# A two-step tanh in the additive attention of a four-layer tower: one ScalarE instruction for 4096 columns, four wide buffers, and one TensorE wait for two steps

## What is computed

```python
k = x @ Wx                                   # (8, 512, 64)
q = x @ Wt
h = jnp.tanh(q[:, :, None, :] + k[:, None, :, :] + bt)   # (8, 512, 512, 64)
e = jnp.exp(jnp.einsum('bijq,qo->bij', h, Wa) + ba[0])
a = e / (jnp.sum(e, axis=-1, keepdims=True) + EPS)
v = jnp.einsum('bij,bjd->bid', a, x)
...
g = jnp.einsum('sd,edh->esh', flat, w_gate)  # the mixture that follows
u = jnp.einsum('sd,edh->esh', flat, w_up)
y = jnp.einsum('esh,ehd->esd', jax.nn.silu(g) * u, w_down)
```

## Time and profile before

| what | value |
|---|---|
| median of 3 runs | 2263.53 us (2260.45 to 2264.91) |
| profiled execution, its own time | 2263.48 us |
| its span, first to last instruction | 2261.7 us |
| busy PE, DVE, ACT, share of the span | 82%, 77%, 58% |
| tanh of 2048 columns (L1944) | 432 instructions |
| the stage's first and last L1944 | start at 700.9 and 1801.8 us |

### The profile page before, as it was taken

The page is one execution under the profiler, slowest core; times in us unless marked ns, Lnnn a source line. Parts: engine busy times, 40 slices in busy tenths (PEclk is TensorE's granted clock), DMA queues, the critical chain, the costliest instruction groups (busy, mean ns, idle before and its releaser), DMA issues. The chain is left out here.

```text
span 2261.7 us, 31852 instructions
## 1 busy us (share of the span) xinstructions
PE 1845.4 (82%) x11804; PEld 950.2 (42%) x11804; DVE 1746.0 (77%) x4911; ACT 1316.9 (58%) x1459; POOL 328.4 (15%) x392
## 2 busy tenths in 40 slices
PE   6999998988766678999899998889999889755930
PEld 3566655766421123344333443333443364333520
DVE  3676557667777789999999999999999889785532
ACT  1222222231226999999999999999999822110410
POOL 6000111010343000000000000000000000057256
PEclk9898998787778899999999999999999999877965
DMA  5501000000001100000000000000000000031732
GB/s 167 182 1 38 18 1 14 1 1 1 1 0 36 66 1 1 1 1 1 1 1 1 1 1 1 1 1 1 1 1 1 1 1 1 0 140 52 229 106 75
DMA packets 39658, 64.98 MB, mean 29 GB/s; under 512 B 7744, under 2 KB 27728, under 8 KB 38736
## 3 DMA queue, kind: packets, MB, share of 16 engines
q1 hardware_dynamic: 30768, 39.86, 5.3%
q0 software_dynamic: 8736, 23.10, 3.3%
HBM read 37.77 MB, written 23.07 MB: 27 GB/s over the span
## 5 line engine op out<-in xcount | busy, mean ns | idle before, releaser
L1944 ACT ACTIVATE KM<-KM 128x2048 f32<-128x2048 f32 x290 | 539.0, 1909 | 8.0 <-DVE KM L1767 8.0
L1767 DVE TENSOR_SCALAR KM<-big 128x512 f32<-128x512 f32 x1160 | 479.5, 479 | 39.3 <-PE bank L2082 33.6
L2082 PE MATMUL bank<-KM,w_a_wa 128*32 128x512 f32 x2736 | 379.1, 628 | 92.4 <-ACT KM L1944 71.0
L191 POOL TENSOR_TENSOR nrstd<-nrstd,minus_half 128x4 f32<-128x4 f32 (+1 forms) x80 | 82.3, 1049 | 1735.7 <-DVE nrstd L168 1735.5
L1944 ACT ACTIVATE aa_args<-aa_args 128x2048 f32<-128x2048 f32 x142 | 266.1, 1910 | 1.5 <-DVE aa_args L1767 1.5
L1767 DVE TENSOR_SCALAR aa_args<-big 128x512 f32<-128x512 f32 x568 | 235.5, 479 | 13.5 <-PE bank L2082 12.9
L2082 PE MATMUL bank<-aa_args,w_a_wa 128*32 128x512 f32 x1360 | 188.8, 629 | 40.7 <-ACT aa_args L1944 26.8
L2082 PEld LDWEIGHTS bank<-KM,w_a_wa 128*32 128x32 f32 x2736 | 54.7, 109 | 243.0 <-ACT KM L1944 140.7
L1941 ACT ACTIVATE KM<-big 128x512 f32<-128x512 f32 x208 | 132.9, 718 | 0.0
L2048 PE MATMUL bank_pair<-XT,rf_wgu 128*128 128x256 f32 x320 | 88.3, 398 | 0.8 <-DVE ST L1839 0.8
L2054 PE MATMUL bank_pair<-XT,rf_wgu 128*128 128x256 f32 x320 | 88.2, 398 | 0.0
(11 more groups left out here) (451 smaller groups left out, 3300.6 us busy)
## 6 DMA issues: line engine op xcount, KB each, us to landing
queues<-zeros SPq DMA_DIRECT2D x1, 8192.0 KB, 24.0
KM<-queues SPq DMA_DIRECT2D x32, 256.0 KB, 3.7
results<-KM POOLq DMA_DIRECT2D x32, 256.0 KB, 3.1
w<-in_w SPq DMA_DIRECT2D x1, 4096.0 KB, 13.1
mf_tv<-in_task_W SPq DMA_DIRECT2D x1, 2048.0 KB, 9.3
la_v<-in_task_W SPq DMA_DIRECT2D x1, 2048.0 KB, 8.0
big<-XN SPq DMA_DIRECT2D x8, 256.0 KB, 2.7
rf_wgu<-in_wgu SPq DMA_DIRECT2D x1, 2048.0 KB, 8.2
```

The costliest lines, as they stand in the source:

```text
L191: self.nc.gpsimd.tensor_tensor(self.m.nrstd[s][:, 0:self.tiles], self.m.nrstd[s][:, 0:self.tiles], self.m.minus_half[:, 0:self.tiles], ALU ...
L1767: last = nc.vector.tensor_scalar(ARG(n, step)[:, cc, :], KU[:, i * T:(i + 1) * T], q, None, ALU.add)
L1944: last = nc.scalar.activation(ARG(n, step), ARG(n, step), ACT.Tanh)
L2082: last = nc.tensor.matmul(m.bank[g][32 * cc:32 * cc + 32, :], w["a_wa"][:, 30 - 2 * k:62 - 2 * k], ARG(n, step)[:, cc, :], start=k == 0, s ...
```

## The change

One ACT instruction now takes the tanh of two steps, an even one and the odd one after it, over 4096 columns. The six buffers of 2048 columns become four of 4096 (`NBUF` = 8 steps). The fourth is where keys and queries used to lie, so keys and queries go to slices of other tiles, the last queries into a tile of zeros that a transfer reads early in the program. ACT raises `th` once for two steps, after both; PE waits for it in even steps only. In the pairs (8, 9), (12, 13) and (16, 17) ACT makes the biased step, then a tanh of 2048 columns for the odd step, then raises `th`; in (22, 23) both are biased. `used` is still raised for each step.

```diff
-    NBUF = 6
+    NBUF = 8
...
-    ARGS = [t[:, 4 * half:4 * half + 4, :] for t in (m.KM[0], m.KM[1], more) for half in range(2)]
-    ARG = lambda n, step: ARGS[(n * CS + step) % NBUF]
+    BOTH = [t[:, :, :] for t in (m.KM[0], m.KM[1], more)] + [m.big[:, o:o + 8 * T].rearrange("p (a t) -> p a t", t=T)]
+    ARG2 = lambda n, step: BOTH[(n * CS + step) // 2 % (NBUF // 2)]
+    ARG = lambda n, step: ARG2(n, step)[:, step % 2 * CG:(step % 2 + 1) * CG, :]
...
-    arg, th, used = sig("arg", CS - len(BIASED)), sig("th", CS), sig("used", CS)
+    arg, th, used = sig("arg", CS - len(BIASED)), sig("th", CS // 2), sig("used", CS)
...
             def tanh(n, i, step):
-                if step in BIASED:
-                    if n * CS + step >= NBUF:
-                        act.wait_ge(used.sem, used.at(n, step - NBUF + 1))
-                    for cc in range(CG):
-                        last = nc.scalar.activation(ARG(n, step)[:, cc, :], KU[:, i * T:(i + 1) * T], ACT.Tanh, bias=query(n, step, cc))
-                else:
-                    act.wait_ge(arg.sem, arg.at(n, args_before(step) + 1))
-                    last = nc.scalar.activation(ARG(n, step), ARG(n, step), ACT.Tanh)
+                if step % 2:
+                    return
+                for k in (step, step + 1):
+                    if k in BIASED:
+                        if n * CS + k >= NBUF:
+                            act.wait_ge(used.sem, used.at(n, k - NBUF + 1))
+                        for cc in range(CG):
+                            last = nc.scalar.activation(ARG(n, k)[:, cc, :], KU[i], ACT.Tanh, bias=query(n, k, cc))
+                plain = [k for k in (step, step + 1) if k not in BIASED]
+                if plain:
+                    act.wait_ge(arg.sem, arg.at(n, args_before(plain[-1]) + 1))
+                    tile = ARG2(n, step) if len(plain) == 2 else ARG(n, plain[0])
+                    last = nc.scalar.activation(tile, tile, ACT.Tanh)
                 last.then_inc(th.sem, 1)
...
+                    if i == PAIRS - 1:
+                        act.wait_ge(m.queues_zero, 16)
...
                     if attention:
-                        pe.wait_ge(th.sem, th.at(n, step + 1))
+                        if step % 2 == 0:
+                            pe.wait_ge(th.sem, th.at(n, step // 2 + 1))
...
+    m.KU = [m.t512c[1][:, 0, :], m.t512c[1][:, 1, :], m.ST[0][:, 2, :], m.ST[1][:, 2, :]]
+    o = NT * (D + 1) + 8 * T
+    m.QU = [m.big[:, o + i * T:o + (i + 1) * T] for i in range(PAIRS - 1)] + [m.zeros[:, :]]
```

More of the change, by code:

```diff
@@ L1014, in retention_and_balanced_experts @@
     AB = m.bank[2:4]
-    o = NT * (D + 1)
-    KU0, QU0 = m.big[:, o:o + T], m.big[:, o + PAIRS * T:o + PAIRS * T + T]
+    KU0, QU0 = m.KU[0], m.QU[0]
     weight = lambda n, e: WT[n // TILES][:, n % NC_ * HE + n // NC_ % HB * E + e:n % NC_ * HE + n // NC_ % HB * E + e + 1]
@@ L1654, in attention_and_experts @@
     o = NT * (D + 1)
-    KU = m.big[:, o:o + PAIRS * T]
-    QU = m.big[:, o + PAIRS * T:o + 2 * PAIRS * T]
+    KU, QU = m.KU, m.QU
     more = ctx.sb("aa_args", [P, 8, T])
-    ARGS = [t[:, 4 * half:4 * half + 4, :] for t in (m.KM[0], m.KM[1], more) for half in range(2)]
-    ARG = lambda n, step: ARGS[(n * CS + step) % NBUF]
+    BOTH = [t[:, :, :] for t in (m.KM[0], m.KM[1], more)] + [m.big[:, o:o + 8 * T].rearrange("p (a t) -> p a t", t=T)]
+    ARG2 = lambda n, step: BOTH[(n * CS + step) // 2 % (NBUF // 2)]
+    ARG = lambda n, step: ARG2(n, step)[:, step % 2 * CG:(step % 2 + 1) * CG, :]
     PROJ = (2, 12, 22)
@@ L1731, in query @@
     def query(n, step, cc):
-        return QU[:, bass.ds(n * P + (step // KS) * GQ + cc * KS + step % KS, 1)]
+        return QU[n // NC_][:, bass.ds(n % NC_ * P + (step // KS) * GQ + cc * KS + step % KS, 1)]
     with nc.Block() as block:
@@ L1766, in arguments @@
                     q = query(n, step, cc)
-                    last = nc.vector.tensor_scalar(ARG(n, step)[:, cc, :], KU[:, i * T:(i + 1) * T], q, None, ALU.add)
+                    last = nc.vector.tensor_scalar(ARG(n, step)[:, cc, :], KU[i], q, None, ALU.add)
                 last.then_inc(arg.sem, 1)
@@ L1955, in project @@
                     act.wait_ge(kq_ps.sem, kq_ps.at(i - 1, 1))
-                    nc.scalar.copy(KU[:, i * T:(i + 1) * T], m.bank[5][:, :]).then_inc(kq_sb.sem, 1)
+                    nc.scalar.copy(KU[i], m.bank[5][:, :]).then_inc(kq_sb.sem, 1)
                     act.wait_ge(kq_ps.sem, kq_ps.at(i - 1, 2))
-                    nc.scalar.activation(QU[:, i * T:(i + 1) * T], m.bank[6][:, :], ACT.Identity, bias=w["a_bt"][:, 0:1]).then_inc(kq_sb.sem, 1)
+                    if i == PAIRS - 1:
+                        act.wait_ge(m.queues_zero, 16)
+                    nc.scalar.activation(QU[i], m.bank[6][:, :], ACT.Identity, bias=w["a_bt"][:, 0:1]).then_inc(kq_sb.sem, 1)
             def iteration(n, i, c, attention=True):
@@ L2782, in build @@
         m = Memory(whole, nc, dram)
+        m.zeros = m.sb("zeros", [P, T])
         workspace(m)
@@ L2786, in build @@
         m.results = nc.dram_tensor("results", (CE * CAP, D), F32).ap()
-        m.zeros = m.sb("zeros", [P, T])
         m.queues_zero = whole.semaphore("queues_zero")
```

## The result

The changed kernel takes 2302.55 us (median of 4, 2301.09 to 2304.16) against 2263.57 before: ratio 1.0167, interval 1.0146 to 1.0188, so 39 us slower. The prediction was 2294, range 2268 to 2318.

What follows compares the result with a forecast made beforehand. A loop of ACT's half and PE's half was taken to bound the stage. 14 periods at +2.15 us (30.1), -0.6 at the start and +1.2 at the end gave +30.7: 2294 us, range 2268 to 2318.

Steps and rivals of the forecast that it cites:

- What bounds the stage: ACT's half, copy to step 24: 23.58 us; PE's half, to step 9's gate: 39.54; then 5.54 to the copy.
- What is saved: On ACT, each merge of two plain tanhs saves 0.09 us; 192 merges are worth 17 us.
- (1): Hand-over at step 24: PE's half begins at 24.76 us after the copy instead of 23.58, +1.18 a period.
- (2): Step 0: the pair (0, 1) is signalled at 16.66 us, PE comes at 16.54; +0.12 a period.
- (3): Steps 12 and 13: PE waits for both before turning the rows; gate to copy 6.39 us against 5.54, +0.85.
- DVE covered: DVE is not on the loop; its closest place, step 27, is covered by 1 us.
- PE's missing waits: Odd steps of PE's half, now without a wait: counted as nothing, up to 0.8 us a period not excluded.
- The rest: Outside the loop: iteration 0 and first half of 1 sum to -0.6 us, end of last iteration +1.2.
- The loop closes 14 times: Each of 14 periods grows by 2.15 us, 68.66 to 70.8, together 30.1 us.
- my case: The main mechanism, the loop lengthened by late signals: 2276 to 2300 us, chance 0.66.
- The clock as a rival: PE's half clock at step 20 falls on steps 22 to 24, 0.7 to 1.6 us each: 2304 to 2316, chance 0.10.
- Every merge counts: Rival: the loop is looser and ACT's 17 us come off, 2246 us (2226 to 2253); chance 0.13.

Runs made afterwards that it cites:

- run 7: Changed kernel with steps 12, 13 and 20 to 31 taken and signalled one by one; ratio 1.0041 to the kernel before.
- run 9: Changed kernel, but after step 11 of iteration 1 only pairs (6, 7), (8, 9), (10, 11), (18, 19) stay together; ratio 0.9963 to the kernel before.
- run 10: Changed kernel with steps 0 to 5, 12, 13 and 20 to 31 taken one by one in every iteration; ratio 0.9978 to the kernel before.
- run 11: As run 9, but steps 12 and 13 share one signal again, no instruction changed; ratio 1.0031 to the kernel before.
- run 12: As run 9, but pair (24, 25) is again one tanh with one signal; ratio 1.0087 to the kernel before.
- run 6: Changed kernel with steps 20 to 31 taken and signalled one by one; ratio 1.0101 to the kernel before.
- run 3: Changed kernel with steps 12 and 13 signalled one by one again, all other pairs as changed; 2284.92 us, ratio 1.0102 to the kernel before.
- run 1: Changed kernel's buffers and moved keys and queries, but one tanh and one signal per step; 2263.34 us, ratio 0.9999 to the kernel before.
- run 8: Changed kernel with the router's exponent on ACT in step 20 instead of 18; ratio 1.0125 to the kernel before.

## Why the prediction was right, point by point

- *What bounds the stage.* Right. The loop of copy, ACT's half, PE's half is what runs 7 and 9 to 12 move about: in runs 9 to 12 most periods are within 0.01 us of the value expected (run 11: 69.43 for 69.42); in runs 6 and 7, where the pair (0, 1) was overlooked, they are 0.6 longer.
- *What is saved.* 0.09 taken, 0.10 measured, within the bounds of 0.05 and 0.195. All of ACT's work is 14 us less where 17 was expected. The figures of the Trainium skill ("ScalarE: Activation LUTs", section "What ACT_TABLE_LOAD costs") come to an estimate of 0.093 saved and 3.598 us for the wide tanh, and the trace agrees (0.10 and 3.611). They are right about the instruction and say nothing of the time here, as run 12 shows.
- *(1) Hand-over at step 24, +1.18.* Measured +1.17 in the first period, with the forecast gap before step 24 (1.00, where I had said 0.9), and +1.30 in the one shown. The pair ends when I had said (24.71 for 24.72). The 0.12 on top is the clock: PE has half clock in steps 20 and 21 of this iteration, between 1248 and 1252 it has 0.62, and is itself done with the gate of step 23 only at 1257.59. So the sign "PE idle for 0.9 before step 24" shows in one period of 14. That gate also reaches ACT late (0.28) and makes the pair (26, 27) late by another 0.13.
- *(2) Step 0, +0.12.* The down projection begins at 1273.16 and step 0 at 1274.38; where nothing waits these are 1.09 apart, so 0.13. Right, and a small term by itself, but run 7 shows that it grows to 0.69 when (1) is taken away. These terms are no constants: each counts only as far as the ones before have not yet made PE late.
- *(3) Steps 12 and 13, +0.85.* Measured +0.86 and shown alone by runs 3 and 11.
- *DVE covered, PE's missing waits worth nothing, places free.* Run 1 shows it for the places. Steps of PE's half still follow at 0.99 without a wait (the gate of step 0 at 1275.37 follows step 0 at 1274.38). DVE's waits for PE to free a buffer, 37.1 us before, are down to 0.7 from 770 us on. ACT had no wait for sums in the middle of the stage.
- *The rest.* Mis-sized: the first two iterations gained 4.8 us where I had 0.6. I took 2 us off the waits at the copies of keys and queries. They were 5.9 us in all, six waits at steps 10, 20 and 30, and all are gone.
- *The loop closes 14 times.* Right, and the first period is the 70.8 that I had for each (70.82); the others are about 71.1 or 72.0. Sum of the 14: 1002.2 against 961.3, +40.9 instead of +30.1. The missing 10.8 us: 13 x 0.26 = 3.4 from the half clock in steps 20 and 21 and its follower, and 8 x 0.93 = 7.4 in the periods where ACT waits before the router's exponent (7.1 of it are the waits themselves).
- *The number.* 2302.55 lies above 2276 to 2300, what I gave for my case alone (its terms add up to 2276 to 2297; the last 3 us have no term), and below the 2304 to 2316 of the clock's. It is inside the stated range since that took in both. The total was helped by two errors of opposite sign, 10.8 too little in the loop and 4.2 too little gained at the start; that they cancel in part is luck.
- *The clock as a rival.* Its mechanism came in part and in another place. I had the half clock at step 20 as hidden and feared it at steps 22 to 24, where PE is waited for next. At steps 20 and 21 it wasn't wholly hidden: it costs about 0.26 a period. And it fell on 14 and 15 as well, after the 2.98 us of standing still that the late signal of (14, 15) makes, and the path from there, router matmul, logits on DVE, exponent on ACT, had 1.8 us of room at full clock (1243.04 to 1244.83) against a delay of 2.8; the prediction had not worked out that path. The step of the prediction that failed is that ACT has no wait from the copy to about step 22: read in the trace before, it was carried over to the changed kernel without a sum. Run 8 shows the cause by moving the exponent behind the next pair.
- *Every merge counts* is refuted by the result, and above all by run 12.

## What to carry to other kernels

Merging two instructions on the fullest engine delays whoever waits for the first, by up to the length of the second, and saves only part of the fixed cost of one instruction; here 1.8 us of delay against 0.1 saved. What decides is not the engine's busy share but, at each signal, how long the consumer still has other work when it comes: write that margin down for all places, including the paths through a third engine, and merge only where it is larger than one instruction. Where the merging engine bounds by itself, as at the start of this stage, the saving comes through. Margins shift when one delay is removed, so test removals together.

## What the runs showed of the hardware

Successive ACT instructions overlap by 0.1 us in the trace: the exponent of two columns lasts 0.19 us (195 ns), but the next tanh starts 0.09 after it (1244.83 and 1244.92). So only half of such a fixed cost can be saved by merging. PE's clock fell to 1.2 GHz (granted 0.50 of full speed) for 6.7 us, from 1307.0 to 1313.7. It fell near the end of a stretch of 2.98 us in which PE stood still (up to 1307.72), and steps 14 and 15 lay in it. Step 14 met it in eight of the fourteen periods, though the same standing still is there in all of them and the instructions repeat. In run 1 and runs 9, 11 and 12, where steps 14 and 15 are apart, PE stands still for 1.28 there and step 14 lasts 1.06 or 1.07 in every iteration from 2 on.
